# Dealing the side work of a selective scan anew over the slots of its scans

## The reference

```
rn    = rmsnorm(layernorm(resid)) * norm_w
skip  = rn @ W_skip                     # 512 -> 1024
x     = silu(conv4(rn @ W_in) + conv_b) # causal, 4 taps, per channel
delta = softplus(x @ W_delta_1 @ W_delta_2 + b)   # 1024 -> 128 -> 1024
B, C  = x @ W_B, x @ W_C                # 1024 -> 16 each
h_l   = h_(l-1) * exp(delta_l * A) + (delta_l * x_l) B_l   # 1024 x 16 states
y_l   = sum_n h_l C_l
out   = resid + ((y + x * W_D) * silu(skip)) @ W_out
```

## Time and profile before

| | us |
|---|---|
| median of 3 runs | 2380.44 (2377.85 to 2384.84) |
| the profiled execution | 2379.91 |
| its span, first to last instruction | 2378.0 |
| first scan starts | 125 |
| chunks 4 to 13 | 1362.0 |
| from the last scan to the end | 155.1 |

### The profile page before, as it was taken

The page is one execution under the profiler, slowest core; times in us unless marked ns, Lnnn a source line. Parts: engine busy times, 40 slices in busy tenths (PEclk is TensorE's granted clock), DMA queues, the critical chain, the costliest instruction groups (busy, mean ns, idle before and its releaser), DMA issues. The chain is left out here.

```text
span 2378.0 us, 35550 instructions
## 1 busy us (share of the span) xinstructions
PE 1958.7 (82%) x11717; PEld 1584.2 (67%) x11717; DVE 1795.4 (75%) x3105; ACT 1669.1 (70%) x3276; POOL 1913.5 (80%) x1192
## 2 busy tenths in 40 slices
PE   5577777898889898898889898898889988797883
PEld 3456666777667676777667686776667776666551
DVE  3377877798697977888697977889697887887522
ACT  2368686877769685787779686786868687787421
POOL 1279898898789797989879897998879898999512
PEclk9988988999999999999999999999999999999996
DMA  4555556665747565674657556574757646555320
GB/s 159 169 178 182 189 177 215 201 216 157 225 151 239 180 215 183 203 229 150 210 175 235 196 186 215 185 228 148 232 169 222 194 154 207 181 183 160 120 71 18
DMA packets 239281, 434.31 MB, mean 183 GB/s; under 512 B 19134, under 2 KB 135418, under 8 KB 239098
## 3 DMA queue, kind: packets, MB, share of 16 engines
q1 hardware_dynamic: 239098, 432.04, 56.9%
HBM read 347.57 MB, written 84.41 MB: 182 GB/s over the span
## 5 line engine op out<-in xcount | busy, mean ns | idle before, releaser
L608 POOL TENSOR_TENSOR hc<-h,c_all 128x1024 f32<-128x1024 f32 x512 | 1205.0, 2365 | 219.5 <-DVE h L953 160.0
L953 DVE TENSOR_TENSOR_SCAN h<-operand,carry,bank 128x512 f32<-128x512 f32 x480 | 597.1, 1271 | 174.1 <-PE bank L1129 142.7
L1134 PE MATMUL y_sum<-ident,hc 128*128 128x128 f32 x4096 | 624.7, 281 | 13.0 <-POOL hc L608 12.7
L1129 PE MATMUL bank<-ident,u_t 128*128 128x128 f32 x2560 | 417.3, 288 | 243.2 <-DVE h L953 219.7
L722 ACT ACTIVATE u_t<-dx_t,b_t 128x256 f32<-128x256 f32 x1280 | 575.0, 499 | 0.5 <-PE bank L1129 0.5
L1129 PEld LDWEIGHTS bank<-ident,u_t 128*128 128x128 f32 x2560 | 312.4, 148 | 375.1 <-issue 240.2
L1134 PEld LDWEIGHTS y_sum<-ident,hc 128*128 128x128 f32 x4096 | 506.1, 146 | 79.8 <-issue 50.2
L592 POOL TENSOR_TENSOR operand<-dx_q,b_all 128x1024 f32<-128x1024 f32 x192 | 454.5, 2367 | 11.0 <-DMA b_all<-bc_dram 11.0
L703 ACT ACTIVATE bank<-delta_q,neg_a 128x512 f32<-128x512 f32 x384 | 262.5, 684 | 263.1 <-DVE h L953 262.7
L703 ACT ACTIVATE operand<-delta_q,neg_a 128x512 f32<-128x512 f32 x640 | 432.9, 714 | 0.0
L953 DVE TENSOR_TENSOR_SCAN h<-bank,carry,operand 128x512 f32<-128x512 f32 x288 | 354.9, 1270 | 33.1 <-POOL operand L592 16.4
(11 more groups left out here) (124 smaller groups left out, 2009.3 us busy)
## 6 DMA issues: line engine op xcount, KB each, us to landing
c_all<-bc_dram SPq DMA_DIRECT2D x256, 512.0 KB, 4.3
b_all<-bc_dram SPq DMA_DIRECT2D x192, 256.0 KB, 5.2
win<-in_L_attn_W_in SPq DMA_DIRECT2D x64, 512.0 KB, 5.7
wskip<-in_L_attn_W_skip SPq DMA_DIRECT2D x64, 512.0 KB, 6.2
x_dram<-x SPq DMA_DIRECT2D x64, 256.0 KB, 4.5
delta_dram<-delta SPq DMA_DIRECT2D x32, 512.0 KB, 7.3
dx_dram<-dx SPq DMA_DIRECT2D x32, 512.0 KB, 7.3
delta_q<-delta_dram SPq DMA_DIRECT2D x32, 512.0 KB, 5.8
```

The source lines that it names most:

```text
L608: nc.gpsimd.tensor_tensor(hc[:, number % 3], h[:, number % 3], c_all[:, j % 2, s % 2:s % 2 + 1].to_broadcast([P, 2, SPAN]), ALU.mult).then ...
L953: nc.vector.tensor_tensor_scan(h[:, number % 3, q], first, second, start, ALU.mult, ALU.add).then_inc(scan_done.sem, 1)
L1129: last = transpose(bank[:, q, b * P:(b + 1) * P], u_t[:, j % 2, b, q * P:(q + 1) * P], ident[:])
L1134: return matmul(to, lhsT=of, rhs=ident[:], is_transpose=True, start=start, stop=stop, skip_group_check=True)
```

## The change

The instructions stay nearly the same; their places change. Plain are now ten slots of 32, the same for every chunk: `PLAIN_SLOTS`. Pairs of the convolution start at `TAPPED` = -5, 1, 6, 10, with halves two slots apart, tanh and x four slots after, the store of x six after, `win` at (-3, late) and (-2, early) relative to them. The norm's load, moments and GpSimd chain stand up to 17 slots earlier (in the step before), and its transposes go to the bank `mixed` instead of `pair_bank`. Low rank, B and C become one product with x as weights and the 160 columns `wlbc` streaming, tokens on partitions; the copy `lbc` serves `make_ut` as B directly, and four transposes bring low and B, C back to the old layout. Skip's two halves stand in two slots. The gate is written over `thg`. Each engine's loop begins one step earlier (step -1), so that negative slots of the first step are reached. Cut to its core:

```diff
-PLAIN_STATES = (0, 3, 5, 8, 11, 13)
-TURNED_STATES = tuple(n for n in range(N) if n not in PLAIN_STATES)
+PLAIN_SLOTS = (0, 2, 4, 7, 10, 13, 18, 22, 25, 29)
+TURNED_SLOTS = tuple(s for s in range(SLOTS) if s not in PLAIN_SLOTS)
+TAPPED = (-5, 1, 6, 10)
...
# SP
-                        if slot == (27 if odd else 17):
+                        if slot == (26 if odd else 17):
                             load_quarter(step + 1, 0)
...
-                            if "norm" in jobs_now and s == 1 and t:
+                            if "norm" in jobs_now and s == -16 and t:
...
-                                    if s == 21 + 2 * eh:
+                                    if s == 22 + 3 * eh:
...
-                                    if s == 23 + 2 * eh:
+                                    if s == 24 + 3 * eh:
...
# GpSimd
-                                if s == 7:
+                                if s == -4:
...
-                                if s == 8:
+                                if s == -3:
...
-                                if s == 9:
+                                if s == -1:
...
-                                    if s == 21 + 2 * eh:
+                                    if s == 22 + 3 * eh:
...
# ScalarE
-                        if slot == 31:
-                            take_dxt(step + 1, 0, 1)
-                        if slot == 29:
-                            take_dxt(step + 1, 0, 0)
+                        if slot in (30, 31):
+                            take_dxt(step + 1, 0, slot - 30)
...
-                                if s == 12:
+                                if s == 6:
                                     if v := due(act, s_ready, t, 1):
...
-                                if s in (25, 26):
-                                    k = 2 * (s - 25)
+                                if s in (13, 15):
+                                    k = s - 13
...
-                                    if s == (20, 20, 22, 22)[p]:
+                                    if s == (21, 21, 24, 24)[p]:
                                         if v := due(act, z_done, t, p + 1):
...
+                                if s == 17:
+                                    if v := due(act, lbc_done, t, 1):
+                                        act.wait_ge(lbc_done.sem, v)
+                                    nc.scalar.activation(lbc[:, (i + 2) // 2 % 2, i % 2 * TB:(i % 2 + 1) * TB],
+                                                         pair_banks[0][:, 0:TB * LBC].rearrange(
+                                                             "p (b n) -> p b n", b=TB),
+                                                         ACT.Copy).then_inc(lbc_ready.sem, 1)
...
# VectorE
-                            if "norm" in jobs_now and s == 5:
+                            if "norm" in jobs_now and s == -8:
...
-                                    if s == 3 * p + 3:
+                                    if s == TAPPED[p] + 4:
...
-                                    if s in (3 * p, 3 * p + 1):
-                                        e = s - 3 * p
+                                    if s in (TAPPED[p], TAPPED[p] + 2):
+                                        e = (s - TAPPED[p]) // 2
...
-                                if s in (30, 43):
-                                    b = s // 43
+                                if s in (31, 41):
+                                    b = s // 41
...
# TensorE
-                    if late and slot in (27, 29):
-                        turn_dx(step + 1, 0, slot // 29)
+                    if (slot, late) in ((28, 0), (29, 1)):
+                        turn_dx(step + 1, 0, late)
...
-                        if "norm" in jobs_now and s in (23, 24) and not late:
+                        if "norm" in jobs_now and s in (11, 13) and late:
...
-                                if (s, late) in ((3 * p - 2, 1), (3 * p - 1, 0)):
+                                if (s, late) in ((TAPPED[p] - 3, 1), (TAPPED[p] - 2, 0)):
+                                    if not p and (v := due(pe, delta_ready, t - 1, PAIRS)):
+                                        pe.wait_ge(delta_ready.sem, v)
...
-                                if s == 10 + p and not late:
+                                if s == (11, 12, 13, 15)[p] and not late:
...
-                                        last = matmul(pair_banks[0][:, 0:T], wd1[:, et, :], x[:, et, :],
-                                                      start=(et == 0), stop=(et == ET - 1))
+                                        for b in range(TB):
+                                            last = matmul(pair_banks[0][:, b * LBC:(b + 1) * LBC],
+                                                          x[:, et, b * P:(b + 1) * P], wlbc[:, et, :],
+                                                          start=(et == 0 and b == 0), stop=(et == ET - 1),
+                                                          skip_group_check=True)
...
-                                if s == (16, 18, 20, 20)[p] and late:
+                                if (s, late) == ((19, 0), (19, 1), (22, 0), (22, 1))[p]:
...
-                                if s == 3 * p + 14:
-                                    e = late
+                                if (s, late) in ((3 * p + 13, 1), (3 * p + 14, 0)):
+                                    e = s - 3 * p - 13
...
-                            b = int(s >= 31)
+                            b = int(s >= 32)
```

More of the change, by code:

```diff
@@ L213, in build @@
         xq_loaded, y_stored = loads_of("xq_loaded", "scan", 2), loads_of("y_stored", "scan", 2)
-        b_loaded = [loads_of(f"b_loaded{k}", "scan", before(PLAIN_STATES, SLOTS) // 2) for k in range(2)]
+        b_loaded = [loads_of(f"b_loaded{k}", "scan", before(PLAIN_SLOTS, SLOTS) // 2) for k in range(2)]
         c_loaded = [loads_of(f"c_loaded{k}", "scan", SLOTS // 4) for k in range(2)]
@@ L459, in store_y @@
                                  y_out[:].rearrange("p (h b) e -> p h b e", h=2)).then_inc(y_stored.sem, 16)
-                for step in range(len(jobs) + 1):
+                for step in range(-1, len(jobs) + 1):
                     odd = (FIRST + step) % 2
@@ L1120, in turn_u @@
                     t, s = now
-                    if not turned_u(place(t, s)[2]):
+                    if not turned_u(s):
                         return
-                    j = before(TURNED_STATES, s)
+                    j = before(TURNED_SLOTS, s)
                     if v := due(pe, ut_ready, t, j + 1):
@@ L1281, in side_work @@
-                                if p == 0 and s == 16 and not late:
-                                    if v := due(pe, bc_ready, t, 1):
-                                        pe.wait_ge(bc_ready.sem, v)
-                                    for b in range(TB):
-                                        last = transpose(pair_banks[1][:, T + b * 2 * N:T + (b + 1) * 2 * N],
-                                                         bc_sb[:, b * P:(b + 1) * P], ident[0:2 * N, 0:2 * N])
-                                    last.then_inc(bt_turned.sem, 1)
@@ new lines, in side_work @@
+                                    if p == PAIRS - 1:
+                                        last.then_inc(lbc_done.sem, 1)
+                                if p == 0 and s == 17 and not late:
+                                    if v := due(pe, lbc_ready, t, 1):
+                                        pe.wait_ge(lbc_ready.sem, v)
+                                    rows_now = lbc[:, (i + 2) // 2 % 2, i % 2 * TB:(i % 2 + 1) * TB]
+                                    for b in range(TB):
+                                        transpose(pair_banks[1][:, b * P:(b + 1) * P], rows_now[:, b, 0:DELTA], ident[:])
+                                    for b in range(TB):
+                                        last = transpose(pair_banks[1][0:2 * N, T + b * P:T + (b + 1) * P],
+                                                         rows_now[:, b, DELTA:], ident[:])
+                                    last.then_inc(lbc_turned.sem, 1)
```

179 lines of the change are left out of this document (80 added, 99 removed).

## The result

The changed kernel takes 2265.8 us (median of 4 runs, 2263.6 to 2271.3) against 2379.1 before (4 runs): a ratio of 0.953 (95% interval 0.951 to 0.954), 113 us less. The forecast was 2270.

A forecast was written before the change was run, and what follows sets the result against it. No engine was full throughout: VectorE led in slots 0 to 10, GpSimd and TensorE in 11 to 21, GpSimd in 22 to 31, plus an odd-chunk stall. Savings of 85, 12, 9, 4 and 0 made 110: 2270, range 2220 to 2346.

The forecast's parts named there:

- The likeliest case: Whole kernel: the parts' savings sum to 110 us, giving 2270, own range 2245 to 2300; chance 0.44.
- The convolution, the largest term: Slots 0 to 10: five convolution halves instead of eight; with related moves -7.6 us, front from 53.8 to 46.2.
- u on GpSimd, -4.6 a chunk: Each chunk: ten u's on GpSimd instead of twelve, at 2.32 us each, take 4.6 us off GpSimd.
- Middle part 41.5: Slots 11 to 21: no engine leads, each waits for the others; bounds 38.9 and 43.2, taken as 41.5 us.
- Back part 40.5: Slots 22 to 31, even chunk: GpSimd at 38.5 us; bounds 38.9 and 43, taken as 40.5.
- The stall of the odd chunk: Odd back part: load lands when it did, shorter work behind it; stall of 9.3 us falls to 3.0.
- Low rank, B and C with x as weights: TensorE: 32 products of 160 columns at 0.15 us each, 4.8 us instead of 6.9, so -2.1 a chunk.
- Ends: Outside the twelve full chunks: fill 4 us less, first two chunks 6 each, last two 4.6 each, drain 0.
- The twelve full chunks: Six even chunks 3.9 us shorter each, six odd ones 10.2 each: 85 us together.
- TensorE held by delta at (24, late): Rival: next chunk's `win` waits for all four deltas, holding up scans; at 9 us a chunk 2396; chance 0.11.
- Each part falls to its fullest engine: Rival: parts of 46.2, 38.9 and 38.9 us, even chunk 124.0, odd 127.0, so 2220 in all; chance 0.18.
- The balanced slots stall each other: Rival: parts of 49.5, 43.2 and 42 us, even chunk 134.7, odd 137.7, so 2348, milder 2310 to 2370; chance 0.24.

The follow-up runs named there:

- the better deal of the slots: The changed kernel with u on GpSimd in slots 0, 3, 5, 8, 10, 13, 18, 22, 25, 29, still ten: 2237.6 us, ratio 0.941.

## Why the prediction was right, and where not

The likeliest case came in (2266 for 2270, its own range 2245 to 2300), and the parts of the chunk moved the way they were forecast. Step by step:

- **The convolution, the largest term: right.** Front 46.2 forecast, "as long as VectorE bounds it"; it takes 46.3 to 47.1 with VectorE busy 42.9 at full clock. The average of chunks 4 to 13 is 47.6; the difference goes with the falls in slot 2. Put back, the convolution makes these fronts 8.8 us longer (forecast for the whole front 7.6), of which 6.5 are VectorE's work, and the middle and back parts 1.9 shorter: 6.9 a chunk, 85 us in all. One sign of the forecast failed: GpSimd's wait for scans in front is not "mostly gone" but 6.2 us in chunk 7, where it was 8.0.

```profile
POOL hc L612 <- DVE h L950: 6.2, 3, 2.4
```

- **u on GpSimd, -4.6 a chunk: its size right (1913.5 to 1840.5 us busy), its worth wrong.** With two more u's the total was the same in one run, whose other slots differ too, and some 6 us longer in the other, not 4.6 a chunk. In the middle the forecast took it off the fullest engine, but that part was also at a clock of 0.93. Which slots have their u on GpSimd counts for more: moving three of them by one slot gives 28 us at the same number, much of it by the clock, and the changed kernel's ten put into the old order cost 27.
- **Middle part 41.5: right at 41.0 with full clock,** 42.2 on average with the falls.
- **Back part 40.5: too high.** The even one takes 38.0. GpSimd was forecast at 38.5 and is at 37.4 in chunk 6, and the part lies within 1 us of it. I had put its lower bound at 38.9, above my own sum for the fullest engine there (38.5; 38.9 is ScalarE's in the middle part) and above what happened. This is the step that was furthest off, 2.5 us in an even chunk and 4.0 in an odd one (with the 3.0 of the stall).
- **The stall of the odd chunk: shorter for other reasons than given.** "So the landing stays where it is" did not hold. The rows, as the earlier trace rows:

```profile
1099.46 0.63 SPq L376 DMA_DIRECT2D dx_q<-dx_dram  x1
```

```profile
1107.69 0.66 PE L1178 MATMUL pair_bank<-ident,dx_q 128*128 128x128 f32 x4 [1.93 <-DMA dx_q<-dx_dram]
```

```profile
1113.19 1.28 DVE L950 TENSOR_TENSOR_SCAN h<-operand,carry,bank 128x512 f32<-128x512 f32 x1 [1.61 <-PE bank L1124]
```

  Counted from the first scan of slot 22 (1079.6; before 1139.0) the load is issued at 19.9 instead of 21.9, the transposes start at 28.1 instead of 30.2, and scan 30 at 33.6 instead of 37.8. In this chunk 5.5 us lie between transposes and scan, in chunks 5, 9, 11 and 13 3.8, as forecast. TensorE's wait for the load is 1.93 us, where it was 6.55. The norm's work in GpSimd's idle time, from which I took 2.5, has no run of its own. What does show: the 2.7 us of this stall that the order on TensorE and ScalarE takes away are worth nothing in the total, since in the next front the clock falls again.
- **Low rank, B and C with x as weights: right.** Eight products of 160 columns take 1.09 us from start to start, 0.136 each; forecast 0.15. So 4.4 us instead of 6.9. That is 0.85 ns a column, as at 256 columns (0.216 each), so the columns set the time and not the loads of the weights. The Trainium skill (TensorE: Matmul & The Clock Gate, section LDWEIGHTS) has a load take its columns over 1.2 in ns, an estimate of 107 ns for 128, which the 136 measured do not contradict. Its own share of the result was not tried.
- **Ends.** Fill -4.4 (forecast 4), the first two chunks -5.4 and -6.2 (6 each), the last two -2.6 and -4.4 (4.6 each), drain -2.2 (0).
- **The twelve full chunks:** even ones (2 to 12) lost 3.4 us on average (forecast 3.9), odd ones (3 to 13) 11.9 (10.2): 91 us, forecast 85.
- **The rivals.** TensorE held by delta at (24, late): refuted. All waits of the input products for delta are 1.9 us in the whole run (4.5 with those of their weight loads), so the 9 us a chunk of this rival did not come:

```profile
L1255 PE MATMUL pair_bank<-rnt,win 128*128 128x256 f32 x1024 | 251.3, 392 | 11.9 <-DVE x L988 8.4 <-ACT delta L817 1.9 <-ACT rnt L782 0.9
```

  Nor does a change of table cost more than its load. ScalarE's timeline, at the second softplus of chunk 7:

```profile
1085.39 1.28 ACT L817 ACT_TABLE_LOAD   x1
1086.68 1.57 ACT L817 ACTIVATE delta<-pair_bank,bdelta 128x256 f32<-128x256 f32 x4
```

  The softplus starts 0.01 us behind the load, and the instruction ahead of the load ends 0.02 us before it. The drain of some 1.38 us of the Trainium skill (ScalarE: Activation LUTs, section What ACT_TABLE_LOAD costs) does not show.
  *Each part falls to its fullest engine* is true of the back part (38.0 with GpSimd at 37.1 on average), not of the middle (41.0 at full clock, with no engine over 38.3 in chunk 6) nor of the front (46.9 with VectorE at 42.9). *The balanced slots stall each other*: slot 8 was its example, with 6.9 us of VectorE; it takes 6.4 on average over chunks 2 to 13, and the front (47.6) and the even back part (38.0) stayed 1.9 and 4.0 us below that case's. The falls of the clock cost some 2 us a chunk, and no case of the forecast had them.

By the runs, of the 113 us 85 are the place of the convolution and 14 the load's slot and the order at the end of the odd chunk; some 14 are left for fill, norm, low rank and the u's, which were not separated. Such shares need not add up, since each run also changes how often the clock falls. Why the sum was so near: 20 us that the clock takes in chunks 4 to 13 were not in it, and a back part forecast some 3.2 us too long, 32 us over the same ten chunks, stood against it. That the miss was 4 us and not 20 or 30 is luck.

## What to carry to other kernels

Read the clock column of the stretches beside their lengths: equal work with two lengths and two clocks is a fall of the clock, and the place to look is the idle time just ahead of it. If TensorE's stream has a hole where another engine is full, move work into it, or fill it with work that is thrown away, and see whether the next part gets shorter. And in a chain of engines that hand work over slot by slot, which slot a piece lies in can count for more than the sum on its engine, as it did here: try a few deals with the same sum before moving work from one engine to another.

## What the runs showed of the hardware

The granted clock of TensorE fell in one chunk and not in another at the same place of the same program. Into the middle part of chunk 6 it did not, with these two stretches ahead of it:

```profile
905.50:909.50 4.00, 2.16 (x16) 1.71 (x16) 3.93 (x9) 4.00 (x10) 3.50 (x9) 1.00 0.33 105
909.50:913.50 4.00, 2.02 (x17) 2.05 (x18) 3.87 (x7) 3.97 (x8) 4.00 (x2) 1.00 0.46 159
```

In chunk 7 it did, with 2.38 and 1.27 us busy ahead of it, and the middle part took 43.4 us instead of 41.3. Adding 1.7 us of useless transposes to each chunk made the kernel 20 us faster, and 2.6 us of them in the better deal of the slots 19 us (2237.6 to 2218.6). I had not expected that work thrown away could pay in a kernel whose TensorE is busy for 85% of the span. The Trainium skill (TensorE: Matmul & The Clock Gate, section HAM oscillation — how this bites in real kernels) tells of a kernel in which each wait of TensorE for a transfer brings the clock down anew; the traces agree in part. In the kernel before, the odd back part with the wait of 6.55 us for a transfer is at 0.92 and the even one without it at 1.00. In the changed kernel it is a wait of 2.89 us for VectorE that stands ahead of the fall in chunk 7.
